# Moving the operands of the large products to multiples of 128 bytes in a transformer block on one core

## The chip, the cores and the metric

The kernel runs on one core of one Trainium2 chip. The metric is the device time of one execution in microseconds (us); lower is better. Three executions of the kernel before took 3674.24, 3675.05 and 3677.36 us, so its median is 3675.05 us.

## The reference

One batch of 8,192 tokens with 512 features goes through a block with two halves. `mod` is made from a condition vector and gives shifts, scales and gates.

```python
h = _layernorm(x) * (1 + ca) + sa
q, k, v = h @ Wq.T, h @ Wk.T, h @ Wv.T            # 1024 columns each: 16 heads of 64
log_decay = -softplus(h @ Wd.T + bd)              # 16 columns
gate = sigmoid(h @ Wg.T)
out = gla_scan(q, k * gate, v, log_decay)         # s = exp(g) * s + k^T v ; o = q s
out = out * rsqrt(mean(out * out) + eps) * norm_w * sigmoid(h @ Wog.T)
x = x + ga * (out @ Wo.T)
h = _layernorm(x) * (1 + cb) + sb
xr, xk = mu * h + (1 - mu) * h_shifted_by_one_token   # once with mu_r, once with mu_k
x = x + gb * sigmoid(xr @ W_r.T) * (relu(xk @ W_k.T) ** 2 @ W_v.T)
```

## The kernel before

**Precision.** Every large product is made in three passes: each operand is held as a rounded part (`_hi`, type fp32r) and the rest (`_lo`, fp32r), and `three_passes` (lines 53 to 57) issues hi x hi on line 55, hi x lo on line 56 and lo x hi on line 57, all into one bank of PSUM. Its arguments `w_hi` and `w_lo` are the stationary operand, 128 columns that are loaded into TensorE by a weight load; `x_hi` and `x_lo` are the moving operand of 256, 264 or 512 columns. So one product over 512 features is 4 steps of k with 3 matmuls, 12 in all. (In the profile the names of a matmul are printed moving operand and stationary operand in no fixed order.)

**Stages.** The tokens are cut into 32 tiles of 256 (two chunks of 128). `prepare` turns, rounds and splits the weights. `attention_pass` then runs over the tiles and writes the attention's output to DRAM; `prepare` runs again for the second set of weights; `output_pass` runs over the tiles for the output product and the second half. In both passes each engine has a program of its own, written out by hand, with semaphores between them.

**attention_pass on TensorE.** For a tile, `project` (line 430) makes eight blocks (b = 0 to 7) of each of g, q and k: the weights are stationary (128 columns of `W`), `h_hi` and `h_lo` move (256 columns). For v it is the other way round: 128 tokens of `h` are stationary, and columns of `W["v"]` move. v's first half and the 16 columns of Wd, which lie behind column 512 in the same rows, are made together: 528 columns in two parts of `VZ` = 264 (b = 0 to 3, for two chunks); v's second half is one part of 512 columns from column 528 on (b = 4, 5). Between these blocks stand, for each of the eight head pairs p of the tile before: the scores `psS` (three passes, `k_hi` and `k_lo` stationary, `q_hi` and `q_lo` moving, 256 columns), a turn of `kg`, and fp32 products with `kw`, `prob`, `state`, `mid` (lines 492 to 510). At a tile's end (p = 0 of the next) TensorE needs the next `h_lo` from VectorE (line 675), which starts when the last v block of the tile is done. ScalarE empties v's banks in `copy_v` (lines 549 to 560).

**output_pass on TensorE.** For a tile: `psG` = h x W_og (tokens stationary, 512 weight columns moving, 48 matmuls), turns of `o_rows` and `x2n`, `psW` = z x W_o (48), `psR` = ra x W_r (24), then k2 (`psW` and `psG`, weights stationary, `xk_hi` and `xk_lo` moving, 256 columns, 48), and `psR` = ra x W_v (24).

**Where the tensors lie.** Tensors are placed in SBUF one behind the other in the order in which the code asks for them, each start rounded up to 32 bytes; a stage's tensors are freed at its end. The weights start at byte 19,072 of a partition, which is 149 x 128. Behind Wq, Wg and Wk (six tensors of 16,384 bytes) `w_v_hi` starts at 117,376 and, with rows of 1,040 columns (4,160 bytes), `w_v_lo` at 134,016; then come `an_norm_x` (150,656), four small tensors of the norm in 256 bytes, and `a_filler` (154,912). In the table "offset" is the remainder of the start by 128; all rows of k but Wv's are a multiple of 128 bytes, so the offset holds for each block of them.

| tensor | start before | offset |
| --- | --- | --- |
| Wq, Wg, Wk, Wog, Wo, W_r, W_k, W_v (parts) | 19,072 and on | 0 |
| Wv, columns from 0, for k = 0, 1, 2, 3 | 117,376 and on | 0, 64, 0, 64 |
| Wv, columns from 264 | | 32, 96, 32, 96 |
| Wv, columns from 528 | | 64, 0, 64, 0 |
| hT, h_hi, h_lo, q, kg, k_hi, k_lo, q_hi, q_lo, v, prob, state, mid, kw and the rest of attention_pass | 154,944 and on | 64 |
| h_hi2, h_lo2, o_rows, z_hi, z_lo, x2n, h2 (output_pass) | 133,760 and on | 0 |
| mix, prev, ra_hi, ra_lo, xk_hi, xk_lo, r_gate (output_pass, behind b_filler at 187,040) | 187,072 and on | 64 |

Of the kernel before, what the change touches and what calls it, by code (L numbers as in the profile page):

```python
# [23 lines left out]
P = 128  # L24
DM = 512
HID = 1024
H = 16
# [6 lines left out]
KD = DM // P  # L34
# [272 lines left out]


KINDS = "gqk"
VZ = (512 + H) // 2  # L310
USES = [(kind, b) for b in range(4) for kind in KINDS] + [("v", b) for b in range(4)]
USES += [(kind, b) for b in range(4, NP) for kind in KINDS] + [("v", 4), ("v", 5)]
BY_ACT = [u for u in USES if u[0] != "k"]
# [2 lines left out]

def attention_pass(nc, t, W, norm, x_v, o_v, h_v, cum_v, cum_b):
    with ExitStack() as ctx:
        def sb(name, shape, dt=F32):
            return ctx.enter_context(nc.sbuf_tensor(name, shape, dt))  # L320
# [2 lines left out]
            return ctx.enter_context(nc.psum_tensor(name, shape, F32))  # L323

        x = norm["x"]
        sb("a_filler", [P, 8])
        hT = sb("hT", [P, KD, T])
        h_hi = sb("h_hi", [P, KD, T], F32R)
        h_lo = sb("h_lo", [P, KD, T], F32R)
# [6 lines left out]
        v = sb("v", [P, NC, HID])  # L336
# [10 lines left out]
        zt = sb("zt", [P, 5, NC, H])  # L347
# [22 lines left out]
        def evacuated(eng, i, u):  # L370

            if u < 0:
                i, u = i - 1, u + NU
                if isinstance(i, int) and i < 0:
                    return
            kind, b = USES[u]
            if kind == "k":
                hold(eng, s["k"], NP * i + b + 1)
            else:
                hold(eng, s["by_act"], NA * i + BY_ACT.index(USES[u]) + 1)  # L380

        def proj_done(i, use):
            return NU * i + USES.index(use) + 1
# [48 lines left out]
        def project(i, kind, b, pe):  # L432

            u = USES.index((kind, b))
            bank = psJ[u % 2]
            evacuated(pe, i, u - 2)
            for k in range(KD):
                if u == 0:
                    pe.wait_ge(s["h_lo"], KD * i + k + 1)
                if kind == "v":  # L440
                    c, at, n = (b // 2, b % 2 * VZ, VZ) if b < 4 else (b - 4, 512 + H, 512)
                    hh, hl = (a[:, k, c * CH:(c + 1) * CH] for a in (h_hi, h_lo))
                    wh, wl = (a[:, k, at:at + n] for a in W["v"])
                    last = three_passes(nc, bank[:, 0:n], hh, hl, wh, wl, k == 0, k == KD - 1)
                else:
                    wh, wl = (a[:, k, b * P:(b + 1) * P] for a in W[kind])
                    last = three_passes(nc, bank[:, 0:T], wh, wl, h_hi[:, k, :], h_lo[:, k, :], k == 0, k == KD - 1)
            last.then_inc(s["proj"], 1)
# [100 lines left out]
        def copy_v(act, i, b):  # L549
            bank = psJ[USES.index(("v", b)) % 2]  # L550
            act.wait_ge(s["proj"], proj_done(i, ("v", b)))
            hold(act, s["gla"], NP * (i - 1) + (4 if b < 4 else 8))
            if b >= 4:
                last = nc.scalar.copy(v[:, b - 4, 512:HID], bank[:, :])
            elif b % 2 == 0:
                last = nc.scalar.copy(v[:, b // 2, 0:VZ], bank[:, 0:VZ])
            else:
                nc.scalar.copy(v[:, b // 2, VZ:512], bank[:, 0:512 - VZ])
                last = nc.scalar.copy(zt[:, 0, b // 2, :], bank[:, 512 - VZ:VZ])
            last.then_inc(s["by_act"], 1)  # L560

        def copy_g(act, i, b):
# [276 lines left out]

def output_pass(nc, t, W, x_v, o_v, h_v, out_v):  # L840

    with ExitStack() as ctx:
        def sb(name, shape, dt=F32):
            return ctx.enter_context(nc.sbuf_tensor(name, shape, dt))
# [11 lines left out]
        x1_old = sb("x1_old", [P, NC, DM])  # L856
        x2n = sb("x2n", [P, NC, DM])
        h2 = sb("h2", [P, KD, T + 1])
        sb("b_filler", [P, 8])
        mix = sb("mix", [P, KD, T])  # L860
        prev = sb("prev", [P, KD, T])
        ra_hi = sb("ra_hi", [P, KD, T], F32R)
# [77 lines left out]
        def pe_tile(pe, i, att, ffn, prep):  # L940
# [14 lines left out]
            if att:  # L955
                pe.wait_ge(s["hl"], 32 * (i + 1))
                for n in range(4):
                    if n < 2:
                        hold(pe, s["relu"], KD * (i - 1))
                    else:  # L960
                        pe.wait_ge(s["sg"], 4 * i + n - 1)
                    rows_product(psG[n % 2], h_hi, h_lo, W["og"], n // 2, n % 2, KD).then_inc(s["og"], 1)
            if att:
# [5 lines left out]
            if att:  # L969
# [3 lines left out]
                for c in range(NC):  # L973
                    ready = [(4 * half, pe, s["zl"], 4 * i + 2 * c + half + 1) for half in range(2)]
                    rows_product(psW[c], z_hi, z_lo, W["o"], c, 0, NP, ready).then_inc(s["wo"], 1)
            if ffn:
# [214 lines left out]
def adaln_gla_block(nc, x, wq, wk, wv, wo, wg, wog, wd, bd, norm_w, w_r, w_k, w_v, mu_r, mu_k, c, wmod, out):  # L1191
    o_rows = nc.dram_tensor("o_rows_dram", (TOK, HID), F32).ap()
    x_v = x.rearrange("a (i c p) d -> (a i) p c d", c=NC, p=CH)
    out_v = out.rearrange("a (i c p) d -> (a i) p c d", c=NC, p=CH)
    cum_dram = nc.dram_tensor("cum_dram", (NT, NC * H, CH), F32).ap()
    cum_v = cum_dram
    cum_b = cum_dram.rearrange("i (c h) t -> i c h t", c=NC)
    h_dram = nc.dram_tensor("h_dram", (NT, P, 2, KD * T), F32).ap()
    h_v = h_dram.rearrange("i p a (k t) -> i p a k t", k=KD)
    o_v = o_rows.rearrange("(i c p) d -> i p c d", c=NC, p=CH)  # L1200
    with ExitStack() as ctx:
        t = {}
        for name, shape, dt in (
            ("ones", [P, P], F32), ("ident", [P, P], F32), ("upto", [P, P], F32), ("after", [P, P], F32),
            ("zeros", [P, 1], F32), ("minus_half", [P, 4], F32), ("bd", [P, H], F32),
            ("mu", [P, 2, KD], F32), ("one_minus_mu", [P, 2, KD], F32), ("norm_w", [P, NP], F32),
            ("silu_c", [P, KD], F32), ("mod", [P, 6, KD], F32), ("ca1", [P, KD], F32), ("cb1", [P, KD], F32),
            ("ga", [P, KD], F32), ("gb", [P, KD], F32),
            ("half", [P, 1], F32),
        ):  # L1210
            t[name] = ctx.enter_context(nc.sbuf_tensor(f"c_{name}", shape, dt))
        small = {"c": c, "wd": wd, "bd": bd, "mu_r": mu_r, "mu_k": mu_k, "norm_w": norm_w}
        wmod_v = wmod.rearrange("(p t) (v n) -> v p t n", t=KD, v=6)

        def pair(ctx2, name, blocks, width):
            return [ctx2.enter_context(nc.sbuf_tensor(f"w_{name}_{part}", [P, blocks, width], F32R))
                    for part in ("hi", "lo")]

        def rows(w, n):
            return w.rearrange("(n r p) d -> n p r d", r=4, p=P)[n]  # L1220

        with ExitStack() as first:
            W = {name: pair(first, name, KD, HID + H if name == "v" else HID) for name in "qgkv"}
            t["wd_hi"], t["wd_lo"] = (a[:, :, 512:512 + H] for a in W["v"])
            jobs = []
            for name, w in (("q", wq), ("g", wg), ("k", wk), ("v", wv)):
                for n in range(2):
                    half = t["half"][:, 0:1] if name == "k" else None
                    at = n * (512 + H) if name == "v" else n * 512
                    cols = [(*(a[:, k, at:at + 512] for a in W[name]), half) for k in range(KD)]  # L1230
                    jobs.append((rows(w, n), None, cols))
                if name == "g":
                    jobs += [(wmod_v[v], v) for v in (SA, CA)]
            norm = norm_parts(nc, first, "an", 1)
            prepare(nc, t, jobs, "p", norm, x_v[0], small)
            attention_pass(nc, t, W, norm, x_v, o_v, h_v, cum_v, cum_b)
        with ExitStack() as second:
            W = {"og": pair(second, "og", KD, HID), "o": pair(second, "o", NP, DM)}
            for name in ("r", "k2", "v2"):
                W[name] = pair(second, name, KD, DM)  # L1240
            cols = {name: [(*(a[:, k, :] for a in W[name]), None) for k in range(KD)] for name in ("r", "k2", "v2")}
            og, o = [], []
            for n in range(2):
                og.append((rows(wog, n), None, [(*(a[:, k, n * 512:(n + 1) * 512] for a in W["og"]), None)
                                                for k in range(KD)]))
                o.append((wo.rearrange("(r p) (n d) -> n p r d", p=P, n=2)[n], t["ga"],
                          [(*(a[:, 4 * n + k, :] for a in W["o"]), t["norm_w"][:, 4 * n + k:4 * n + k + 1])
                           for k in range(4)]))
            mod = {v: (wmod_v[v], v) for v in (GA, GB, SB, CB)}

            jobs = [mod[GA], mod[GB], og[0], o[0], og[1], o[1], mod[SB], mod[CB],
                    (rows(w_v, 0), t["gb"], cols["v2"]), (rows(w_r, 0), None, cols["r"]), (rows(w_k, 0), None, cols["k2"])]
            prepare(nc, t, jobs, "s")
            output_pass(nc, t, W, x_v, o_v, h_v, out_v)
# [24 lines left out]
```

## Time and profile before

| | |
| --- | --- |
| median of three executions | 3675.05 us |
| the profiled execution's own time | 3674.58 us |
| its span in the trace | 3672.8 us |
| TensorE matmuls busy (25,349 of them) | 3596.5 us, 98% of the span |
| weight loads busy | 3339.3 us, 91% |
| VectorE / ScalarE / GpSimd busy | 2145.5 / 1546.0 / 464.7 us |
| granted TensorE clock, mean of the span | 0.991 |

The profile is one execution. A row of a group view gives: line of the code, engine, operation, tiles written and read, shape, count, then busy time in us and the mean duration of one in ns, and what the engine had idled for before. A matmul's duration is the time from its start to its modelled end and is longer than the distance to the next one, since matmuls overlap; the distance ("pace" below) is read from the starts in the timeline. A row of the timeline gives start and duration in us, then the same names. A row of the windows view gives the stretch and its length, then for each engine its busy time and how many instructions, the granted clock (1.00 is 2.4 GHz), and the DMA share and rate.

### The profile page before, as it was taken

The numbers are of one execution on the slowest core, as the hardware profiler recorded it, in microseconds if no ns is written. First come the engines' busy times: TensorE is split into PE (matmuls) and PEld (weight loads), VectorE is DVE, ScalarE is ACT, GpSimd is POOL, SyncE is SP. The second block draws the span as 40 slices with busy tenths as digits, with TensorE's granted clock in tenths as the row PEclk, the third lists the DMA queues.
The fourth block names the chain that finished last, engine by engine and source line by source line (L and its number), as shares of the span: only waits on it lengthen the run. The fifth ranks groups of instructions, "written<-read, shape, count | busy, mean of one in ns | idle before, by whom it ended". The sixth has DMA issues, their size and how long they took to land. (4 is left out here: it accounts for less than half of the span.)

```text
span 3672.8 us, 73725 instructions
## 1 busy us (share of the span) xinstructions
PE 3596.5 (98%) x25349; PEld 3339.3 (91%) x25349; DVE 2145.5 (58%) x5207; ACT 1546.0 (42%) x3904; POOL 464.7 (13%) x883
## 2 busy tenths in 40 slices
PE   7999999999999999999999997899999999999998
PEld 7999999999999999999999997688888888888887
DVE  4555555555555555555555556566566655666566
ACT  4445445445545445445445453333332323233332
POOL 0111111111111111111111111100000000000000
PEclk8999999999999999999999999899999999999999
DMA  4222322322322322322232223412221122212220
GB/s 156 76 60 65 81 60 58 87 62 56 87 63 55 86 64 54 81 71 54 75 77 54 75 71 87 162 69 71 77 91 69 69 80 85 75 69 74 75 91 23
DMA packets 206044, 274.89 MB, mean 75 GB/s; under 512 B 13968, under 2 KB 146080, under 8 KB 206000
## 3 DMA queue, kind: packets, MB, share of 16 engines
q1 hardware_dynamic: 206000, 274.31, 25.6%
q8 instruction: 27, 0.44, 0.1%
q14 instruction: 17, 0.14, 0.0%
HBM read 189.84 MB, written 84.41 MB: 75 GB/s over the span
## 5 line engine op out<-in xcount | busy, mean ns | idle before, releaser
L813 POOL TENSOR_TENSOR k_lo<-kg,k_hi 128x256 fp32r<-128x256 f32 x256 | 186.7, 729 | 1501.1 <-ACT q_hi L588 1501.1
L609 ACT ACTIVATE decay<-cum_rows,w_cur 128x128 f32<-128x128 f32 x1024 | 327.8, 391 | 20.6 <-POOL cum_rows L807 12.7
L55 PE MATMUL psJ<-h_hi,w_g_hi 128*128 128x256 f32 x1024 | 314.7, 307 | 8.3 <-DVE h_lo L675 4.6
L577 ACT COPY q<-psJ 128x256 f32<-128x256 f32 x256 | 95.5, 373 | 501.1 <-PE psJ L57 501.1
L55 PE MATMUL psJ<-h_hi,w_q_hi 128*128 128x256 f32 x1024 | 304.4, 297 | 0.0
L683 DVE SCALAR_TENSOR_TENSOR kg<-gate,psJ 128x256 f32<-128x256 f32 x256 | 107.8, 421 | 333.0 <-PE psJ L57 305.5
L56 PE MATMUL psJ<-h_lo,w_q_hi 128*128 128x256 f32 x1024 | 286.2, 279 | 0.0
L57 PE MATMUL psJ<-h_hi,w_k_lo 128*128 128x256 f32 x1024 | 286.1, 279 | 0.0
L56 PE MATMUL psJ<-h_lo,w_g_hi 128*128 128x256 f32 x1024 | 285.9, 279 | 0.0
L57 PE MATMUL psJ<-h_hi,w_q_lo 128*128 128x256 f32 x1024 | 285.8, 279 | 0.0
L55 PE MATMUL psJ<-h_hi,w_k_hi 128*128 128x256 f32 x1024 | 285.6, 279 | 0.0
L56 PE MATMUL psJ<-h_lo,w_k_hi 128*128 128x256 f32 x1024 | 285.6, 279 | 0.0
L57 PE MATMUL psJ<-h_hi,w_g_lo 128*128 128x256 f32 x1024 | 285.4, 279 | 0.0
L725 DVE SCALAR_TENSOR_TENSOR mid<-state,w_cur,psK 64x64 f32<-64x64 f32 x512 | 143.3, 280 | 234.1 <-PE psK L492 230.4
L691 DVE TENSOR_TENSOR q_lo<-q,q_hi 64x256 fp32r<-64x256 f32 x512 | 263.6, 515 | 11.3
L499 PE MATMUL psO<-v,prob 128*128 128x64 f32 x2048 | 261.6, 271 | 0.0
L55 PE MATMUL psJ<-w_v_hi,h_hi 128*128 128x264 f32 (+1 forms) x768 | 254.3, 331 | 0.0
L499 PEld LDWEIGHTS psO<-v,prob 128*128 128x128 f32 x2048 | 248.9, 192 | 2.1
L56 PE MATMUL psJ<-w_v_lo,h_hi 128*128 128x264 f32 (+1 forms) x768 | 246.7, 321 | 0.0
L57 PE MATMUL psJ<-w_v_hi,h_lo 128*128 128x264 f32 (+1 forms) x768 | 246.4, 321 | 0.0
L1030 ACT ACTIVATE og<-psG 128x512 f32<-128x512 f32 x128 | 76.5, 598 | 358.2 <-PE psG L57 358.2
L1113 DVE TENSOR_TENSOR o_rows<-o_rows,og 128x512 f32<-128x512 f32 x128 | 88.6, 692 | 228.7 <-ACT og L1030 228.7
(226 smaller groups left out, 10601.8 us busy)
## 6 DMA issues: line engine op xcount, KB each, us to landing
cum_rows<-cum_dram SPq DMA_DIRECT2D x256, 256.0 KB, 5.4
o_rows_dram<-o SPq DMA_DIRECT2D x256, 128.0 KB, 1.8
o_rows<-o_rows_dram SPq DMA_DIRECT2D x32, 1024.0 KB, 5.4
an_norm_x<-in_L_attn_x_dram SPq DMA_DIRECT2D x32, 512.0 KB, 3.9
h_dram<-h_hi SPq DMA_DIRECT2D x32, 512.0 KB, 2.7
h_dram<-h_lo SPq DMA_DIRECT2D x32, 512.0 KB, 3.8
h_hi<-h_dram SPq DMA_DIRECT2D x32, 512.0 KB, 3.7
h_lo<-h_dram SPq DMA_DIRECT2D x32, 512.0 KB, 4.6
```

The lines of the kernel that those rows point to most:

```text
L55: nc.tensor.matmul(out, w_hi, x_hi, start=first, stop=False)
L56: nc.tensor.matmul(out, w_hi, x_lo, start=False, stop=False)
L57: return nc.tensor.matmul(out, w_lo, x_hi, start=False, stop=last)
L499: nc.tensor.matmul(psO[:, c, h * DH:(h + 1) * DH], prob[:, 2 * c + h, :], v[:, c, p * P + h * DH:p * P + (h + 1) * DH], start=True, stop=True)
L577: nc.scalar.copy(q[:, b, :], psJ[USES.index(("q", b)) % 2][:, 0:T]).then_inc(s["by_act"], 1)
L609: last = nc.scalar.activation(decay[:, 2 * c + h, :], cum_rows[:, p % 4, 2 * c + h, :], ACT.Exp, bias=w_cur[:, 3, c, 2 * p + h:2 * p + h + ...
L683: nc.vector.scalar_tensor_tensor(out=kg[:, b, :], in0=gate[:, b % 2, :], scalar=1.0, in1=psJ[USES.index(("k", b)) % 2][:, 0:T], op0=ALU.ad ...
L691: last = nc.vector.tensor_tensor(q_lo[r, :, h, :], q[r, p, :].rearrange("p (c t) -> p c t", c=NC), q_hi[r, :, h, :].bitcast(F32), ALU.subt ...
L725: last = nc.vector.scalar_tensor_tensor(out=mid[r, r], in0=state[r, p, r], scalar=w_cur[r, 2, 0, 2 * p + h:2 * p + h + 1], in1=psK[r, 2, r ...
L813: nc.gpsimd.tensor_tensor(k_lo[:, :], kg[:, p, :], k_hi[:, :].bitcast(F32), ALU.subtract).then_inc(s["k_lo"], 1)
L1030: nc.scalar.activation(og[:, n % 2, :], psG[n % 2][:, :], ACT.Sigmoid).then_inc(s["sg"], 1)
L1113: nc.vector.tensor_tensor(rows, rows, og[:, n % 2, :], ALU.mult).then_inc(s["z"], 1)
```

## The change

Three things. `a_filler` and `b_filler`, unused tensors of 32 bytes, become 96 bytes. Wv's rows are padded from 1,040 to 1,056 columns (4,224 bytes = 33 x 128), with 16 unused columns between Wd's 16 and v's second half, which now starts at column 544. And v's first half with Wd is made as 256 and 272 columns instead of twice 264. No instruction is added or taken away; shapes change in these v blocks and in the copies of `copy_v` alone.

```diff
-VZ = (512 + H) // 2
+V_PARTS = ((0, 256), (256, 256 + H), (544, 512))
@@ attention_pass
-        sb("a_filler", [P, 8])
+        sb("a_filler", [P, 24])
@@ project
-                    c, at, n = (b // 2, b % 2 * VZ, VZ) if b < 4 else (b - 4, 512 + H, 512)
+                    c = b // 2 if b < 4 else b - 4
+                    at, n = V_PARTS[b % 2 if b < 4 else 2]
@@ copy_v
             elif b % 2 == 0:
-                last = nc.scalar.copy(v[:, b // 2, 0:VZ], bank[:, 0:VZ])
+                last = nc.scalar.copy(v[:, b // 2, 0:256], bank[:, 0:256])
             else:
-                nc.scalar.copy(v[:, b // 2, VZ:512], bank[:, 0:512 - VZ])
-                last = nc.scalar.copy(zt[:, 0, b // 2, :], bank[:, 512 - VZ:VZ])
+                nc.scalar.copy(v[:, b // 2, 256:512], bank[:, 0:256])
+                last = nc.scalar.copy(zt[:, 0, b // 2, :], bank[:, 256:256 + H])
@@ output_pass
-        sb("b_filler", [P, 8])
+        sb("b_filler", [P, 24])
@@ adaln_gla_block
-            W = {name: pair(first, name, KD, HID + H if name == "v" else HID) for name in "qgkv"}
+            W = {name: pair(first, name, KD, 1056 if name == "v" else HID) for name in "qgkv"}
@@
-                    at = n * (512 + H) if name == "v" else n * 512
+                    at = n * V_PARTS[2][0] if name == "v" else n * 512
```

## Rows read from the trace of the kernel before

**Rows 1.** Windows view: three stretches (attention, between the passes, output).

```profile
core 0: us, PE busy (x) PEld busy (x) DVE busy (x) ACT busy (x) POOL busy (x), PEclk, DMA share, GB/s
200.00:2200.00 2000.00, 1994.23 (x16356) 1946.84 (x16355) 1145.32 (x3054) 985.92 (x2716) 369.22 (x721) 1.00 0.27 68
...
2285.00:2345.00 60.00, 35.38 (x176) 30.57 (x177) 33.87 (x64) 20.88 (x35) 10.09 (x13) 0.71 0.66 236
...
2450.00:3600.00 1150.00, 1150.00 (x6023) 982.61 (x6022) 706.57 (x1479) 362.86 (x727) 37.95 (x55) 1.00 0.21 76
```

**Rows 2.** Waits of TensorE's matmuls: total us, times, longest us.

```profile
PE s_mod L130 <- DVE s_sums L275: 20.4, 4, 12.2
...
PE psJ L55 <- DVE h_lo L675: 4.6, 16, 2.2
```

**Rows 3.** Groups by shape, TensorE, 2450 to 3600 us (output_pass).

```profile
L56 PE MATMUL psW<-w_o_lo,z_hi 128*128 128x512 f32 x448 | 174.3, 389 | 0.0
...
L56 PE MATMUL psG<-w_og_lo,h_hi 128*128 128x512 f32 x440 | 171.3, 389 | 0.0
...
L56 PE MATMUL psR<-w_r_lo,ra_hi 128*128 128x512 f32 x224 | 88.6, 396 | 0.0
...
L56 PE MATMUL psR<-w_v_lo,ra_hi 128*128 128x512 f32 x223 | 88.1, 395 | 0.0
```

**Rows 4.** Timeline, TensorE: first matmul of each block of a tile in output_pass.

```profile
3005.69 0.40 PE L55 MATMUL psR<-w_r_hi,ra_hi 128*128 128x512 f32 x1
...
3011.28 0.28 PE L55 MATMUL psW<-xk_hi,w_k_hi 128*128 128x256 f32 x1
...
3016.94 0.40 PE L55 MATMUL psR<-w_v_hi,ra_hi 128*128 128x512 f32 x1
...
3022.53 0.39 PE L55 MATMUL psG<-w_og_hi,h_hi 128*128 128x512 f32 x1
...
3033.43 0.27 PE L951 MATMUL psG<-c_ident,o_rows 128*128 128x128 f32 x1
```

**Rows 5.** Timeline, attention_pass: start and end of 23, then of 24 matmuls.

```profile
1026.88 0.28 PE L56 MATMUL psJ<-h_lo,w_q_hi 128*128 128x256 f32 x1
...
1029.60 0.39 PE L510 MATMUL psO<-mid,q 128*128 128x128 f32 x2
...
1059.45 0.28 PE L55 MATMUL psJ<-h_hi,w_q_hi 128*128 128x256 f32 x1
...
1062.17 0.28 PE L55 MATMUL psS<-q_hi,k_hi 128*128 128x256 f32 x1
```

**Rows 6.** Groups by shape, TensorE, 1026.90 to 1029.55 us.

```profile
L56 PE MATMUL psJ<-h_lo,w_k_hi 128*128 128x256 f32 x4 | 1.1, 281 | 0.0
```

**Rows 7.** Groups by shape, TensorE, 1059.45 to 1062.10 us.

```profile
L56 PE MATMUL psJ<-h_lo,w_q_hi 128*128 128x256 f32 x4 | 1.1, 276 | 0.0
```

**Rows 8.** Groups by shape, whole trace.

```profile
L56 PE MATMUL psJ<-h_lo,w_q_hi 128*128 128x256 f32 x1024 | 286.2, 279 | 0.0
...
L57 PE MATMUL psJ<-h_hi,w_g_lo 128*128 128x256 f32 x1024 | 285.4, 279 | 0.0
...
L499 PE MATMUL psO<-v,prob 128*128 128x64 f32 x2048 | 261.6, 271 | 0.0
...
L492 PE MATMUL psK<-v,kw 128*128 128x128 f32 x1024 | 156.0, 274 | 4.4 <-DVE kw L712 4.4
...
L57 PE MATMUL psJ<-w_v_hi,h_lo 128*128 128x264 f32 x512 | 145.6, 284 | 0.0
...
L57 PE MATMUL psS<-q_hi,k_lo 128*128 128x256 f32 x512 | 145.1, 283 | 0.0
L56 PE MATMUL psS<-q_lo,k_hi 128*128 128x256 f32 x512 | 144.4, 282 | 0.0
...
L57 PE MATMUL psJ<-w_v_hi,h_lo 128*128 128x512 f32 x256 | 100.9, 394 | 0.0
...
L925 PE MATMUL psT<-c_ident,x2n 128*128 128x128 f32 x256 | 33.2, 273 | 0.0
```

**Rows 9.** Timeline, TensorE: a wait at the start of a tile.

```profile
1003.30 0.38 PE L55 MATMUL psJ<-h_hi,w_g_hi 128*128 128x256 f32 x1 [0.16 <-DVE h_lo L675]
```

## Prediction

> **What bounds the kernel now.** I read the stages first, then TensorE's waits, then the groups of matmuls, then the starts of single ones. In the windows view the reader is to see that matmuls are under way in 1994.2 of 2000 us of the attention stage and in all 1150 us of the output stage, at the full clock, and that only the short stretch between the passes is mostly something else [rows 1]. TensorE's waits say the same: the largest, 20.4 us, lies between the passes, and in attention the one of note is for h_lo at the start of a tile, 4.6 us in 16 places [rows 2]. So the end is set by how many matmuls are issued and how far apart they start. A change that alters only addresses can act through that distance, the pace, and hardly through anything else.
>
> Does the pace depend on addresses? The trace holds a trial of it. In output_pass, W_o and z, and W_og and h_hi2, all have offset 0. The 48 matmuls of a W_og block start between 3022.53 and 3033.43 us, 227.1 ns apart; those of ra x W_r, as wide and with the same order of operands, but with the stationary ra at offset 64, start between 3005.69 and 3011.28 us: 24 in 5.59 us, 232.9 ns; ra x W_v, 24 from 3016.94 to 3022.53 us, also 232.9 ns [rows 4]. The modelled durations agree over 1150 us: 389 ns for both aligned groups, 395 to 396 ns for both with ra [rows 3]. k2, where only the moving xk is at 64, takes 48 matmuls of 256 columns from 3011.28 to 3016.94 us, 117.9 ns each [rows 4]; half of 227.1 would be 113.5.
>
> In attention_pass h is at 64 everywhere, and two paces occur. At 1026.88 us 23 matmuls take 2.72 us (118.3 ns, duration 281 ns), at 1059.45 us 24 take 2.72 us (113.3 ns, duration 276 ns) [rows 5 to 7]. A block keeps the pace with which it settles after the fp32 products ahead of it. The aligned 512-column blocks show one pace only. I read this as: with both operands at offset 0 the slow pace does not hold, and 113.3 ns is the pace of 256 columns.
>
> **The change part by part.** First the addresses. Wv's rows of 4,224 bytes make w_v_hi and w_v_lo 256 bytes longer each, 512 in all, a multiple of 128, so a_filler stays at offset 32 (155,424) and its 96 bytes put hT at 155,520 = 1,215 x 128. All that lies behind goes from 64 to 0. v's parts start at 0, 1,024 and 2,176 bytes of a row, all multiples of 128. b_filler at 187,040 and its 96 bytes put mix at 187,136 = 1,462 x 128. So after the change every operand of three_passes is at 0.
>
> a) g, q, k: 3 x 3 x 1,024 = 9,216 matmuls. Their mean durations are 279.5 and 278.7 ns (286.2 and 285.4 us by 1,024) [rows 8]; seven other groups lie between these or carry the restart below. 279.1 lies at 0.62 of the way from 276 to 281 [rows 6, 7], so about 62% run slow. The slow pace costs 4.6 ns (117.9 less 113.3) [rows 4, 5]. One in 12, the first of a block, restarts TensorE after something else and is left out: 8,448 x 0.62 x 4.6 ns = 24.1 us.
>
> b) v's first half: 1,536 matmuls of 264 columns, 284.4 ns (145.6 us by 512) [rows 8]. Aligned ones would lie on the line from 276 at 256 to 389 at 512 columns [rows 3, 7], 0.44 ns a column: 276 for 256 and 283.1 for 272, mean 279.5. 4.9 x 1,536 = 7.5 us. That one part is narrower and one wider cancels.
>
> c) v's second half: 768 matmuls at 394.2 ns (100.9 us by 256) [rows 8] against 389 [rows 3]: 5.2 x 768 = 4.0 us.
>
> d) ra x W_r and ra x W_v: 1,536 matmuls; 5.8 ns by the starts [rows 4], 6.3 by the durations [rows 3]. 6.05 x 1,536 = 9.3 us.
>
> e) k2: 1,536 matmuls, 117.9 to 113.3 ns [rows 4, 5]: 4.6 x 1,536 = 7.1 us. No aligned block of this shape is in the trace; its gain lies between 0 and this.
>
> f) The scores psS: both operands at 64, 283.4 and 282.0 ns [rows 8] against 276 [rows 7], 6.7 ns. A sixth of the 1,536, the first of a slot, is a restart: 1,280 x 6.7 = 8.6 us.
>
> g) The fp32 products and turns of attention_pass (lines 476, 492, 499, 501, 510), 4,608 matmuls whose operands also go to 0. Lines 499 and 492 have 271 and 274 ns, the aligned turn of x2n 273 [rows 8]. I take 0, and 2 ns each either way as bounds (the farther of the two rows): -9 to +9 us.
>
> h) ScalarE's copies of 264 and 248 columns become 256 and 256; all engines but TensorE are busy under 60% [rows 1], so they are covered. Should ScalarE become late, 64 such copies with 8 columns more are worth well under 1 us. No DMA, no wait and no queue is moved.
>
> The sum is 60.6 us. Of this, part stays hidden. At the start of a tile TensorE stands waiting for h_lo [rows 9], and the chain to h_lo runs through ScalarE and VectorE from the end of the last v block; what TensorE saves between the two (six scores and most of a g block, some 6 x 6.7 + 11 x 2.9 = 72 ns) only makes it wait longer: 32 x 72 ns = 2.3 us. Nothing else is near: VectorE has 1145 us in 2000 [rows 1]. Net gain 58 us, 1.6%. Against the profiled execution's own 3674.58 us this gives 3616.6; the median is 0.5 us above that execution, so 3617 us.
>
> The Trainium skill speaks against all of this. Its page "SBUF — State Buffer", section "Specifications (TRN2)", gives cachelines of 16 bytes, and its section "Operand start alignment" asks of a start only that it is a multiple of the element size (a rule, it says, about legality, with nothing timed). Every start named above was a multiple of 32 already, so by it nothing changes and the time stays at 3675. The trace disagrees with it: 227.1 against 232.9 ns at equal shape [rows 4].
>
> **The rivals.**
>
> *No effect (3675).* What separates the blocks is not the offset but what else runs beside them, or the phase in which they start; that attention_pass runs at 113.3 ns with h at 64 [rows 5] speaks for it. Against it: W_og and W_r differ in little else, in every tile, over 1150 us [rows 3]. The whole gain is then 0.
>
> *The two paces stay in attention (3641).* Which pace g, q and k settle into is decided by the moment of the restart and not by the offset; the other terms come as worked out. Then a) is missing: 3617 + 24 = 3641. For it: both paces occur at one and the same set of addresses [rows 5]. Against it: k2, also at 64, never shows the fast one in rows 4, and the aligned groups' mean of 389 leaves no room for a second pace.
>
> *Slower: equal offsets collide (3697).* The scores are the only 256-column products with both operands at the same offset, and they are the slowest of that width, 6.7 ns over the fast pace [rows 7, 8]. If what counts is that the weight load and the moving operand read from the same offset, g, q and k come to 120.0 ns from a mean of 116.2 (113.3 + 0.62 x 4.6): 3.8 x 8,448 = +32 us; v's first half +1.8 x 1,536 = +2.8, k2 +2.1 x 1,536 = +3.2, scores 0; c) and d) still give 13.3. Together +25, less what the wait for h_lo hides, some 2: 3675 + 23 = 3698, say 3697. It decides once the pace of aligned 256-column matmuls is above 118.0 ns: an excess x over 113.3 changes the time by 12,800 x less 61 us, which is zero at 4.7 ns. Against it: at 512 columns equal offsets of 0 are the fastest [rows 3], though there the weight load has twice the time.
>
> **How the numbers follow.** Forecast, 3605 to 3632 by the bounds of g) and by e) falling away: 0.74. The two paces stay: 0.12. No effect: 0.07. Slower: 0.07. About 0.2%, 7 us, is what a measurement of this kernel can tell from no change. The range for 8 in 10 takes the forecast with its bounds and most of the second case: 3603 to 3648. Faster by over 0.2%: 0.74 + 0.12 = 0.86; same 0.07; slower 0.07.
>
> **What would show it.** In the profile after, with the first row of rows 8 as the model: g, q and k on lines 56 and 57 at a mean of 276 ns, ra x W_r and ra x W_v at 389, k2 at about 276, v's 512 columns at 389, v's first half as two groups of 276 and 283, scores near 276. Blocks of W_o and W_og stay at 389. The wait for h_lo grows by some 2 us. The prediction is wrong in a) if g, q and k keep a mean between 277 and 281; wrong as a whole if the psR groups stay at 395; and the slower rival is right if g, q and k come to 282 or more.

## The result and the profile after

The changed kernel takes 3708.6 us (median of four executions, 3705.1 to 3711.1), the kernel before 3674.65 us (four executions, 3674.2 to 3677.4): a ratio of 1.009 with a 95% interval of 1.0078 to 1.0102. It is 0.9% slower, where a gain of 58 us was forecast, and lies outside the forecast range. The profiled execution took 3705.1 us, its span is 3703.4 us, 30.6 us longer than before.

The windows view after, three stretches as in [rows 1]:

```profile
core 0: us, PE busy (x) PEld busy (x) DVE busy (x) ACT busy (x) POOL busy (x), PEclk, DMA share, GB/s
200.00:2200.00 2000.00, 1994.69 (x16145) 1949.46 (x16144) 1127.06 (x3012) 971.57 (x2676) 364.48 (x712) 1.00 0.26 67
...
2285.00:2345.00 60.00, 34.25 (x223) 29.80 (x224) 44.89 (x100) 20.64 (x49) 13.71 (x24) 0.82 0.60 199
...
2450.00:3600.00 1150.00, 1150.00 (x6003) 984.19 (x6002) 704.85 (x1475) 358.38 (x719) 38.61 (x56) 1.00 0.21 75
```

The reader is to see that TensorE is as busy as before and at the same clock, and gets less done: 16,145 matmuls in the 2,000 us of attention against 16,356 [rows 1]. (The middle row is not to be compared: attention ends some 30 us later, so the same 60 us hold other work.) No wait of the two passes has grown in sum; the one for h_lo, 4.6 us in 16 places before [rows 2], is now smaller:

```profile
PE psJ L55 <- DVE h_lo L676: 2.6, 1, 2.6
```

So the pace changed. The groups by shape, whole trace after, for the groups of [rows 8]:

```profile
L56 PE MATMUL psJ<-h_lo,w_q_hi 128*128 128x256 f32 x1024 | 289.8, 283 | 0.0
L56 PE MATMUL psJ<-h_lo,w_k_hi 128*128 128x256 f32 x1024 | 289.8, 283 | 0.0
...
L57 PE MATMUL psS<-q_hi,k_lo 128*128 128x256 f32 x512 | 145.4, 284 | 0.0
...
L57 PE MATMUL psJ<-w_v_hi,h_lo 128*128 128x512 f32 x256 | 100.8, 394 | 0.0
...
L57 PE MATMUL psJ<-w_v_hi,h_lo 128*128 128x272 f32 x256 | 74.4, 291 | 0.0
...
L57 PE MATMUL psJ<-w_v_hi,h_lo 128*128 128x256 f32 x256 | 72.3, 282 | 0.0
```

283 ns stands where 276 was forecast and 279.5 was [rows 8]. In the timeline, 23 matmuls of a q and k block, from the first row to the second:

```profile
1026.38 0.28 PE L56 MATMUL psJ<-h_lo,w_q_hi 128*128 128x256 f32 x1
...
1029.14 0.27 PE L511 MATMUL psO<-mid,q 128*128 128x128 f32 x1
```

That is 2.76 us, 120.0 ns each, against 118.3 and 113.3 ns in [rows 5]. And the groups of the output stage (2450 to 3600 us) that answer to [rows 3]:

```profile
L56 PE MATMUL psG<-w_og_lo,h_hi 128*128 128x512 f32 x448 | 174.3, 389 | 0.0
...
L56 PE MATMUL psR<-w_v_lo,ra_hi 128*128 128x512 f32 x224 | 88.5, 395 | 0.0
...
L56 PE MATMUL psR<-w_r_lo,ra_hi 128*128 128x512 f32 x224 | 88.4, 395 | 0.0
```

ra now lies at offset 0 like its weights, and still has 395 ns and not 389.

**Where the 30.6 us are.** From here on the pace is the distance between the starts of neighbouring matmuls, taken over all of a block's matmuls in a trace; means leave out distances over 130 ns (over 250 at 512 columns), which are restarts and waits. Each distance counts for the matmul that starts it. Sums of these distances, after less before: g +8.8, q +10.3, k +11.9 us, together +31.0; v's first half +1.4, its second half -0.6; scores -0.3; fp32 products and turns +0.6. Attention as a whole is 32.1 us longer. In the output stage k2 +3.3, ra x W_r -0.3, ra x W_v -0.7, W_og -1.5, W_o +0.2: the stage +1.0. The stretches before, between and behind the passes give -2.5 back.

### The profile page after: what moved, and what is told of

Read it like the earlier page. It is cut to its first block and busy times, and to the rows that moved or that the text cites. A ratio compares the mean times of both kernels' runs of the same rounds, so it can differ in the third digit from the quotient of the medians.

```text
span 3703.4 us, 73725 instructions
## 1 busy us (share of the span) xinstructions
PE 3628.4 (98%) x25349; PEld 3374.8 (91%) x25349; DVE 2143.0 (58%) x5207; ACT 1544.5 (42%) x3904; POOL 464.9 (13%) x883
## 5 line engine op out<-in xcount | busy, mean ns | idle before, releaser
L55 PE MATMUL psJ<-w_v_hi,h_hi 128*128 128x256 f32 (+2 forms) x768 | 254.2, 331 | 0.0
L57 PE MATMUL psJ<-w_v_hi,h_lo 128*128 128x256 f32 (+2 forms) x768 | 247.5, 322 | 0.0
L56 PE MATMUL psJ<-w_v_lo,h_hi 128*128 128x256 f32 (+2 forms) x768 | 246.2, 321 | 0.0
L1114 DVE TENSOR_TENSOR o_rows<-o_rows,og 128x512 f32<-128x512 f32 x128 | 88.6, 692 | 227.2 <-ACT og L1031 227.2
```

The lines of the kernel that those rows point to most:

```text
L55: nc.tensor.matmul(out, w_hi, x_hi, start=first, stop=False)
L56: nc.tensor.matmul(out, w_hi, x_lo, start=False, stop=False)
L57: return nc.tensor.matmul(out, w_lo, x_hi, start=False, stop=last)
L1114: nc.vector.tensor_tensor(rows, rows, og[:, n % 2, :], ALU.mult).then_inc(s["z"], 1)
```

## The experiments

Where nothing else is said, a time below is one execution; the kernel before took between 3673.3 and 3677.5 us in all its executions, so a difference of up to 4 us says nothing. Changes of a stage are taken against the one trace of the kernel before. "By 128" or "by 512" means the remainder of a division by that number of bytes.

Two theories of what an address does to the pace. Theory A: each operand's own offset by 128 counts. Theory B: the distance between the moving operand's start and the stationary one's counts. "Distance" is the start of h less that of the weights, by 512 bytes, in g, q and k; in k2 it is xk less W_k; for ra (stationary) it is ra less its weights. Before: 192 for h, 64 for xk, 64 for ra. After: 256, 128, 128.

### The same distances at other addresses

```diff
             ("half", [P, 1], F32),
+            ("ahead", [P, 16], F32),
```

> The kernel before, with an unused tensor of 64 bytes ahead of all weights: every operand moves by 64 bytes (W to offset 64, h, q_hi, k_hi, ra and xk to offset 0), and no distance between two of them changes. Theory A, the offset of each operand by 128 decides: now h and xk are at 0 and W at 64, so the paces change, g, q and k away from the present mean of 116.0 ns by some ns, W_og and W_o (now both at 64) away from 227 ns towards 233. Theory B, only the distance between the moving and the stationary operand decides: all paces stay within 0.3 ns, the time at 3675 us within 3.

Measured: 3676.4 us, the kernel before beside it 3674.3. Means of g, q, k 115.7, 116.0 and 116.0 ns (before 115.7, 116.1, 116.2), k2 117.8 (117.8), W_og and W_o 227.5 (227.1, 227.2), ra x W_r 233.3 (233.3). The offsets by 128 of all these operands have changed and no mean by more than 0.4 ns. A group by shape of this run:

```profile
L56 PE MATMUL psJ<-h_lo,w_k_hi 128*128 128x256 f32 x1024 | 285.5, 279 | 0.0
```

Theory A falls as an account of the means. h_hi starts at byte 159,104 here, at offset 0.

The means are not all. The two rows of this run that answer to the first pair of [rows 5], the same 23 matmuls of the same tile:

```profile
1028.78 0.28 PE L56 MATMUL psJ<-h_lo,w_q_hi 128*128 128x256 f32 x1
...
1031.40 0.27 PE L510 MATMUL psO<-mid,q 128*128 128x128 f32 x1
```

They take 2.62 us, 113.9 ns each, where the kernel before has 118.3, though the distance between the operands is the same. Over the 32 tiles q and k of block b = 2 went from 117.6 ns to 114.9 and 114.6, those of b = 1 from 114.3 and 113.9 to 116.6 and 116.5; in the mean of all blocks this cancels. In v's second half, where nothing cancels, the mean went from 231.7 to 232.5 ns, and in the block between lines 501 and 510 the fourth matmul is 228 ns from the next in the kernel before and 239 here, in each of the 32 tiles to about 1 ns. So which block gets which pace does hang on something else that 64 bytes for all weights and activations change. Their absolute place is one candidate; their distance from `c_ident` is another, since it and the other constants lie ahead of the added tensor and stay where they were (the expectation says that every operand moves). No run separates the two.

### The two fillers alone

```diff
-        sb("a_filler", [P, 8])
+        sb("a_filler", [P, 24])
...
-        sb("b_filler", [P, 8])
+        sb("b_filler", [P, 24])
```

> The kernel before with the two fillers of 96 bytes alone; Wv's rows and the parts of 264 columns stay. h lies 64 bytes further from Wg, Wq, Wk than before (distance by 512: 256 in place of 192), as in the changed kernel. Both theories A and B: g, q, k at 120 ns as in the changed kernel, attention longer by about 31 us, 3706 us in all, output stage +1. Rival C, the padding and the new parts of v are what disturbs g, q and k (other phases behind them): near 3675 us here.

Measured: 3708.1 us against 3674.3; attention +32.6 us, output stage +1.6. The same group, whole trace:

```profile
L56 PE MATMUL psJ<-h_lo,w_k_hi 128*128 128x256 f32 x1024 | 289.8, 283 | 0.0
```

h_hi starts at 159,104 as in the run with everything shifted; only the weights start 64 bytes lower. Those 64 bytes of distance are worth 32 us.

### The padding and v's new parts alone

```diff
-        sb("a_filler", [P, 24])
+        sb("a_filler", [P, 8])
...
-        sb("b_filler", [P, 24])
+        sb("b_filler", [P, 8])
```

(against the changed kernel)

> The changed kernel with both fillers back at 32 bytes: Wv padded and v in parts of 256 and 272, h at offset 64 again. Since the padding moves h by 512 bytes, the distance from W to h is that of before by 512 (192) but not by 1024. Theory B with a period of 512: g, q, k with the two paces of before, mean 116.0 ns, time 3675 us, give or take 3 for v. With a period of 1024: another pace. Theory A: as before too, since all offsets by 128 are as before. Rival C: near 3705.

Measured: 3674.35 us against 3674.28; g, q, k together 116.0 ns, v's first half 188.2 us in all (before 189.5), its second 183.9 (183.5). Rival C falls, and the padded rows and new parts are worth nothing measurable in either direction. Nor do the 512 bytes by which the padding moves h, which change its distance by 1024. With the run before this one, the whole loss belongs to the two fillers.

### Equal starts

```diff
-        sb("a_filler", [P, 8])
+        sb("a_filler", [P, 88])
...
-        sb("b_filler", [P, 8])
+        sb("b_filler", [P, 120])
```

> The kernel before with a_filler of 352 and b_filler of 480 bytes: h and W, and ra, xk and W, start at the same place by 512, as W_og and h_hi2, and W_o and z, already do. Theory B: ra x W_r and ra x W_v fall from 233 to 227 ns (10 us of the output stage), since that is the distance of W_og; for 256 columns the distance 0 is seen only in the scores, at 118 to 120 ns, so k2 comes to 118 to 120 and g, q, k to about 120 (+31 us). Theory A: all operands at offset 0, so everything as in the changed kernel: ra at 233, g, q, k at 120.

Measured: 3701.8 us against 3674.3; attention +32.8, output stage -6.8. Distance 0 gives g, q, k 119.6 ns in the mean, as 256 does, k2 119.8, and ra x W_r 226.7, ra x W_v 228.7. Here ra, h and all weights have offset 0, exactly as in the changed kernel, where ra x W_r took 232.9: only the distance by 512 differs, 0 against 128. So 0 is the good distance at 512 columns with stationary tokens and a bad one at 256 columns with moving tokens.

### Steps of 32, 96 and 128 bytes

Three kernels, which differ from the kernel before in the size of both fillers: 16, 32 and 40 elements in place of 8.

```diff
-        sb("a_filler", [P, 8])
+        sb("a_filler", [P, 16])
...
-        sb("b_filler", [P, 8])
+        sb("b_filler", [P, 16])
```

> The kernel before with fillers of 64 bytes: h, xk and ra 32 bytes further, their distance from the weights 96 by 128 in place of 64. Theory B1: the pace falls and rises evenly with how far the distance is from 0 by 128 (64 the best): g, q, k between 116 and 120 ns, about 118 (+17 us), k2 about 119. Theory B2: only exact multiples of 128 collide: g, q, k stay at 116.0, k2 at 117.8 or below. Rival D: nothing but the phase at a block's start counts, and any new layout gives a pace of its own anywhere between 113.3 and 120.

> The kernel before with fillers of 128 bytes: distance 32 by 128. Theory B1: as at 96, about 118 ns for g, q, k, about +17 us. Theory B2: 116.0. By either, this kernel and the one with 64 bytes agree within 1 ns if the distance counts the same in both directions; if weight load and moving operand run through memory in one direction, a lead and a lag of 32 bytes may differ.

> The kernel before with fillers of 160 bytes: distances 128 bytes larger than before, the same by 128 (64) but not by 256. Period of 128: g, q, k at 116.0 ns and k2 at 117.8, 3675 us within 3. Period of 256 or more: other paces, g, q, k off by over 1 ns. ra x W_r, 512 columns wide, is expected at 233 ns by a period of 128; its one good distance so far is 0 by 512.

Measured: 3698.5, 3682.4 and 3684.7 us against 3675.0. g, q, k 118.3, 116.8 and 117.7 ns; k2 119.9, 118.7 and 117.7; ra x W_r 233.9, 233.3 and 229.0. Neither B1 nor B2 holds as written: distance 224 is 2.3 ns above the pace of 192, distance 288 only 0.8. The first two kernels, 32 bytes on either side of 256, differ by 1.5 ns, so the distance does not count the same in both directions. The period of 128 falls: distances 192 and 320 have 116.0 and 117.7 ns, and ra x W_r, expected at 233, has 229.0. Rival D in its plain form, any layout its own pace, is not needed either, since equal distances gave equal means in the runs above.

### ra alone, and two more distances for h

```diff
-        sb("b_filler", [P, 8])
+        sb("b_filler", [P, 120])
...
+        sb("xk_filler", [P, 16])
         xk_hi = sb("xk_hi", [P, KD, T], F32R)
```

> The kernel before with b_filler of 480 bytes and a second filler of 64 bytes between ra and xk: ra starts where W_r and W_v do by 512, xk keeps its distance of 64. Attention untouched. Theory B: ra x W_r at 226.8 and ra x W_v at 227 to 229 ns as in the kernel with equal starts, k2 at 117.8 as before: the output stage 9 to 10 us shorter, 3665 us. If the gain at ra needed xk at distance 0 too (phase carried over), it is lost: 3675.

Measured: 3666.0 us against 3675.0; output stage -9.0, attention +1.7 with its paces unchanged. ra x W_r 226.7, ra x W_v 229.3, k2 117.9. Groups of the output stage, 2450 to 3600 us:

```profile
L56 PE MATMUL psR<-w_v_lo,ra_hi 128*128 128x512 f32 x224 | 87.4, 390 | 0.0
...
L56 PE MATMUL psR<-w_r_lo,ra_hi 128*128 128x512 f32 x224 | 87.1, 389 | 0.0
```

The gain that the prediction's d) had promised is there, at distance 0 and not at offset 0 alone. In the next two, a_filler has 128 and 72 elements and xk_filler 48:

> h at a distance of 160 from the weights by 512 (32 by 128, as k2 had at 118.7 ns and g, q, k at 116.8 with 288); ra at 0, xk at 192. If what counts is the distance by 128 alone: g, q, k at 116.8 ns, attention +8 us on before, output -9: 3674 us. If distances of one remainder by 128 differ, as 192 (116.0) and 320 (117.7) do: between 115 and 120.

> h at a distance of 448 (64 by 128 and 192 by 256). If the period is 256: two paces and a mean of 116.0 as at 192, attention as before, output -9: 3666 us. If 448 settles at 118 as 320 did, by the phase at the restart: 117.7 ns, +18 in attention, 3684 us.

Measured beside the kernel before at 3676.6: 3683.0 and 3664.5 us. Distance 160: 118.0 ns (attention +20.0 us), which the distance by 128 alone would have put at 116.8. Distance 448: 116.0 ns, the same as 192 to 0.1 ns, and again with two paces in the same blocks. With 0 and 256 this is the second pair 256 bytes apart that agrees; in both pairs v's second half agrees too (distances as for h: 231.7 ns at 192 and 448, 233.0 at 0 and 256).

### The best layout, timed

a_filler as before, b_filler 120 elements, xk_filler 48.

> The best layout so far: attention as before (h at 192), ra at distance 0, xk at 192 in place of 64 (k2 at 117.6 ns, as with fillers of 160 bytes). Theory of the distance: the output stage 9 us shorter than before, 3665 us, 0.25% below the kernel before and 1.2% below the changed one.

Measured: 3665.8 us against 3676.6, a ratio of 0.997 with a 95% interval of 0.9958 to 0.9981. It beats both kernels, the kernel before by 10.8 us. By its trace the output stage is 9.6 us shorter; ra x W_r has 226.7 ns, ra x W_v 229.2, and k2 stays at 117.8, so the gain is that of ra.

### One weight tensor apart

```diff
+                if name == "q" and part == "lo":
+                    ctx2.enter_context(nc.sbuf_tensor("q_filler", [P, 16], F32))
```

(in `pair`, between w_q_hi and w_q_lo)

> The kernel before with 64 unused bytes between w_q_hi and w_q_lo: all behind, h too, moves by 64 bytes, so h_hi and h_lo are at distance 256 from w_q_hi alone (as in the changed kernel) and at 192 from w_q_lo, Wg and Wk (as before). Theory of the distance: g and k stay at 115.7 and 116.2 ns though h is at offset 0; q rises to between 117 and 119.5, 3 to 10 us in all. If a matmul is slowed by the weight load that runs while it streams (the next one's): lines 57 and 55 are slow (the loads of w_q_hi for lines 55 and 56 run beside them) and line 56, beside which w_q_lo is loaded, is nearer 116. If it is its own stationary operand: lines 55 and 56 slow, 57 not. Theory of the offset: h at offset 0 makes g, q and k alike, 119 or more.

Measured: 3689.0 us against 3675.2; g 116.7 ns, q 118.1, k 117.9. By line, q has 117.9, 117.6 and 118.7 ns on lines 55, 56 and 57, k 117.5, 117.5 and 118.7. This run settles little. k has its good distance of 192 and is slow nevertheless, and g, which follows other matmuls than q, has risen by 1.0 ns at the same distance. So the distance of a block's own operands does not settle its pace alone. k follows q without a restart, and the rows of [rows 5] show that either pace, once there, holds. Which of the two reads beside a matmul, its own operand's or the next one's, can't be read from lines 55 to 57, since a slow q no longer alternates. That q alone is hit, as was expected, did not come true.

### Taking the aligned blocks apart, and distances 128 and 96

```diff
+        sb("og_filler", [P, 16])
         h_hi = sb("h_hi2", [P, KD, T], F32R)
```

with a_filler and b_filler of 120 elements; in the second kernel a_filler 112, b_filler 120, xk_filler 48.

> Output pass: a filler of 64 bytes ahead of h_hi2, so that h_hi2 and z lie 64 bytes further, at the distance of 64 from their weights that ra has in the kernel before; b_filler holds ra and xk at 64. Theory of the distance: W_og and W_o rise from 227 to 233 ns, 3,072 matmuls, +18 us of the output stage. If these blocks owe 227 ns to something else: no change there. Attention: h at distance 128. If distance 128 is as in k2 (119.9 ns): g, q, k at 119.9, +32 us, 3725 us in all; if it is 117 or less, k2 and these blocks differ.

> h at distance 96, ra at 0, xk at 192. If distance 96 is as in k2 (119.9 ns): g, q, k at about 119.9, attention +32, output -10, 3697 us. If blocks that restart after the fp32 products settle otherwise than k2: between 115.7 and 118.5, 3665 to 3685 us.

Measured: 3719.1 and 3694.8 us against 3673.3. In the first the output stage is 18.1 us longer, W_og 233.4 and W_o 233.3 ns in place of 227.1 and 227.2. Its groups, 2450 to 3600 us:

```profile
L56 PE MATMUL psW<-w_o_lo,z_hi 128*128 128x512 f32 x441 | 174.1, 395 | 0.0
...
L56 PE MATMUL psG<-w_og_lo,h_hi 128*128 128x512 f32 x432 | 170.6, 395 | 0.0
```

All four 512-column blocks of this pass can thus be put near 389 or at 395 ns by the distance. Attention: distance 128 gives 118.8 ns, between the two values that the expectation weighed (119.9 as in k2, and 117); distance 96 gives 119.7, as k2.

The mean paces in ns, by distance modulo 256 (for k2 no pair 256 bytes apart was run):

| distance | g, q, k | k2 |
| --- | --- | --- |
| 0 | 119.6 (two runs, and the changed kernel) | 119.8 |
| 32 | 116.8 | |
| 64 | 117.7 | 117.8 |
| 96 | 119.7 | 119.9 |
| 128 | 118.8 | 119.9 |
| 160 | 118.0 | 118.7 |
| 192 | 116.0 (five runs, and the kernel before) | 117.7 to 117.8 |
| 224 | 118.3 | |

## Why the prediction was wrong

**What held.** That TensorE's pace is the thing the change moves: of the 33.1 us by which the two passes are longer, the blocks' distances in g, q, k and k2 are 34.3, the stretches outside the passes give 2.5 back, and no wait of the passes grew in sum. The places of h and ra by 128 held too. (Two slips change nothing: the four small tensors of the norm fill 160 bytes and not 256, `a_filler`'s start is right; and the bounds of g) and e) around 3617 give 3608 to 3633 and not 3605 to 3632.)

**The step that failed** is the sentence "with both operands at offset 0 the slow pace does not hold, and 113.3 ns is the pace of 256 columns". The trial in [rows 3, 4] was between blocks that differ in two things at once: W_og and h_hi2 have equal offsets by 128, and they are also a whole multiple of 512 bytes apart. The prediction named the first; the runs show that the second decides the mean. Same offset, other distance: ra x W_r at 232.9 ns in the changed kernel and 226.7 at distance 0. Other offset, same distance: no mean changed by more than 0.4 ns for these blocks and for g, q and k in the kernel shifted by 64 bytes. And 113.3 ns is one of two paces of 256 columns at distance 192, not the pace that aligned operands settle at: no layout brought g, q and k under 115.9 ns in the mean. The address table of the kernel before held what was needed to see it.

**Term by term.** a) forecast -24.1 us, measured +31.0: the two paces of distance 192, with 42% of the matmuls at 113 to 115 ns, give way to 120 ns at distance 256, where 2% are that fast. b) forecast -7.5, measured +1.4. c) forecast -4.0, measured -0.6; in the rows of Wv the distance changes with k, so no one filler gives it a good distance throughout. d) forecast -9.3, measured -1.0; the term was available, at distance 0. e) forecast -7.1, measured +3.3: the pace of 113.3 for k2 was taken from g, q, k, and no run of k2, at six distances, had a mean under 117.6. f) forecast -8.6, measured -0.3: q_hi and k_hi moved together, so their distance could not change; this alone could have been read off the table. g) +0.6, within its bounds. The 2.3 us that the wait for h_lo was to hide did not arise.

**The rival that came true** is "equal offsets collide", given 0.07. Its 120.0 ns for g, q and k, its +32 us for them and its +3.2 for k2 came out as 119.6, +31.0 and +3.3. Its total of 3697 is 12 us too low, since it still allowed 13.3 us for c) and d), which came to 1.6. Its evidence, that the scores are slow, was read rightly: they have equal starts by 512. That a matmul of 256 columns behaves otherwise than one of 512 stood in it as the point on which it decides, and was then discounted because the 512-column blocks were fast. Its rule was still luck in part: at distance 96, where the two offsets differ, g, q and k are just as slow (119.7 ns), and at distance 128, where they are equal, a little less so (118.8).

**What stays open.** Why 192 and 448 admit two paces is not settled. Within blocks of one and the same distance the fast pace followed some restarts and the slow one others [rows 5]: in the kernel before, the 44 q blocks whose first matmul is 206 or 207 ns from the second all run fast afterwards, and of the 173 with 200 to 202 ns 147 run slow. The shift of everything by 64 bytes changed which blocks are fast, and the run with w_q_hi apart shows a pace carried on from q to k. That the cause is a clash of the weight load with the read of the moving operand is argued and not shown: no run separated the two. What speaks for it is that the mean goes by the distance between them, and that they run side by side, as the timeline of the changed kernel has it:

```profile
1027.69 0.28 PE L55 MATMUL psJ<-h_hi,w_k_hi 128*128 128x256 f32 x1
1027.70 0.19 PEld L56 LDWEIGHTS psJ<-h_lo,w_k_hi 128*128 128x128 f32 x1
1027.82 0.28 PE L56 MATMUL psJ<-h_lo,w_k_hi 128*128 128x256 f32 x1
1027.82 0.19 PEld L57 LDWEIGHTS psJ<-h_hi,w_k_lo 128*128 128x128 f32 x1
```

In these rows the load for the next matmul starts within 0.01 us of the present matmul.

## What to carry to other kernels

Where TensorE is busy throughout and each matmul has a weight load of its own, tabulate the distance between the two operands' starts by 256 and by 512, not only each one's offset, and scan it with a filler: here it was worth about 3% of the pace (116.0 to 119.7 ns, 226.7 to 233.9 ns), and a good distance for one shape (0 at 512 columns) was a bad one for another (256). When two groups of a trace are compared as a trial, list everything in which they differ before naming the cause. A filler sized for one tensor moves all that is placed behind it, so give tensors of different needs fillers of their own, as ra and xk here.

## What the runs showed of the hardware

In this kernel the mean pace of fp32r matmuls with 128 stationary columns depends on the distance between the operands: 116.0 to 119.9 ns at 256 columns, 226.7 to 233.9 at 512, at full clock and with TensorE hardly idle. With 64 bytes more for all weights and activations, and their distances kept, the means of g, q, k, k2, W_og, W_o and ra x W_r stay within 0.4 ns, while v's second half changes by 0.8, and single blocks of q and k change from one of their two paces to the other. 64 bytes more in the two fillers make the kernel 34 us longer, 32.6 of them in attention.

The Trainium skill's page "SBUF — State Buffer", section "Who interferes with whom", gives TensorE two independent read ports, one for the moving operand and one for the weight load, and says that it never waits on another. The measurement differs from what that suggests: the two operands' places relative to each other change the pace by 3%. Whether the two reads meet in something that they share, no run shows. Its section "Operand start alignment" asks only for a multiple of the element size and says that nothing there was timed. All starts here keep to it, and the layouts tried here range from 3664.5 to 3719.1 us.
